# Dequantisation in the first stage alone, and the bf16 parts of the point weights made by GpSimd

## What is computed

```
x = x + xattn0(layernorm(x), ctx, ctx, Wq, bq, Wk, bk, Wv, bv, Wo, bo)
x = x + ffn0(layernorm(x), w_freq_real, w_freq_imag, bias)
x = x + xattn1(layernorm(x), ctx, ctx, w_value, b_value, w_off, b_off, w_attw, b_attw, w_out, b_out)
x = x + ffn1(layernorm(x), w_gate, w_up, w_down)
```

```
s = max(max|w| over the block / 7, 1e-12)
wq = clip(round(w / s), -8, 7) * s
```

## Time and profile before

| what | value |
|---|---|
| median of three runs | 871.84 us (866.13, 871.84, 871.96) |
| the profiled execution | 868.69 us |
| its span | 866.2 us |
| its mean granted TensorE clock | 0.941 |
| busy: TensorE, VectorE, ScalarE, GpSimd | 727.4, 639.0, 465.5, 249.8 us |

### The profile page before, as it was taken

How to read it: one execution, slowest core, us unless ns; L and a number is a source line. 1 busy time by engine, 2 the same in 40 slices (tenths; PEclk the granted TensorE clock), 3 DMA queues, 4 the chain that set the end, 5 groups by cost and what they waited for, 6 DMA issues and landing times.

```text
span 866.2 us, 10711 instructions
## 1 busy us (share of the span) xinstructions
PE 727.4 (84%) x3599; PEld 485.6 (56%) x3599; DVE 639.0 (74%) x1184; ACT 465.5 (54%) x818; POOL 249.8 (29%) x198
## 2 busy tenths in 40 slices
PE   4999998799977788767999987999979990039998
PEld 4878886578766567523455553444434440018887
DVE  3577799966798579955999975877569997993333
ACT  2444455455334668855655512344379959934441
POOL 3000000576784112365676720000023320000000
PEclk9999999799999999889999997999999995559999
DMA  8900000050143300000000000000014339501111
GB/s 279 349 12 1 1 1 0 1 135 1 30 139 85 35 1 1 2 1 1 2 2 1 1 2 0 1 0 1 0 73 163 158 147 403 219 0 37 49 52 58
DMA packets 32122, 52.87 MB, mean 61 GB/s; under 512 B 3523, under 2 KB 27331, under 8 KB 30918
## 3 DMA queue, kind: packets, MB, share of 16 engines
q1 hardware_dynamic: 30256, 50.62, 17.7%
q10 hardware_dynamic: 1814, 1.59, 0.6%
HBM read 35.34 MB, written 16.84 MB: 60 GB/s over the span
## 4 chain that ended last, share of the span: by engine, by line
PE 41%; ACT 11%; DVE 8%; issue 4%; DMA 1%; POOL 0%; SPq 0%; DVEq 0%; ACTq 0%; POOLq 0%
PE pair L1544 10%; PE pair L1591 10%; PE pair L1472 4%; PE pair L1440 4%; PE pair L1455 3%; DVE wide L2085 3%; PE pair L1483 2%; ACT upq L1081 2%; ACT g2q L1087 2%; PE pair L1332 2%; PE pair L1335 2%; ACT wide L1050 1%; DVE peak L1997 1%; PE pair L1569 1%; DMA ups<-up_far 1%
## 5 line engine op out<-in xcount | busy, mean ns | idle before, releaser
L1932 DVE SCALAR_TENSOR_TENSOR hat<-pair,hat 128x1024 f32<-128x1024 f32 x64 | 78.0, 1218 | 29.5 <-ACT hat L970 18.2
L970 ACT ACTIVATE hat<-pair 128x1024 f32<-128x1024 f32 x64 | 65.5, 1024 | 60.9 <-PE pair L1440 60.9
L1569 PE MATMUL pair<-xqs,wuT 128*128 128x512 f32 x192 | 84.6, 601 | 4.7 <-ACT up_stage L1037 4.7
L1544 PE MATMUL pair<-xqs,wgT 128*128 128x512 f32 x192 | 85.4, 603 | 0.0
L1591 PE MATMUL pair<-wdT,hid 128*128 128x256 f32 x384 | 83.1, 379 | 0.4 <-DVE hid L2133 0.4
L723 POOL TENSOR_TENSOR hat<-hat 128x1024 f32<-128x1024 f32 x30 | 70.7, 2357 | 41.3 <-DVE hat L1932 41.3
L1591 PEld LDWEIGHTS pair<-wdT,hid 128*128 128x128 f32 x384 | 72.9, 190 | 11.1 <-DVE hid L2133 1.2
L1569 PEld LDWEIGHTS pair<-xqs,wuT 128*128 128x128 f32 x192 | 36.8, 194 | 51.3 <-issue 51.1
L1152 PE MATMUL pair<-wT,ft_sb 128*128 128x256 f32 x256 | 63.8, 392 | 0.0
L623 POOL TENSOR_TENSOR rstd<-lnt,half 128x8 f32<-128x8 f32 (+2 forms) x15 | 26.4, 1760 | 129.5 <-DVE lnt L1635 129.5
L1102 ACT ACTIVATE hid<-wide,unit 128x768 f32<-128x768 f32 x32 | 32.5, 1026 | 57.2 <-DVE hid L2133 43.7
(11 more groups left out here) (243 smaller groups left out, 1711.8 us busy)
## 6 DMA issues: line engine op xcount, KB each, us to landing
up_far<-up_stage SPq DMA_DIRECT2D x24, 512.0 KB, 2.6
ups<-up_far SPq DMA_DIRECT2D x8, 1536.0 KB, 6.9
x_sb<-in_x_dram SPq DMA_DIRECT2D x8, 512.0 KB, 7.4
c_sb<-in_ctx_dram SPq DMA_DIRECT2D x8, 512.0 KB, 8.7
ctx<-in_ctx_dram SPq DMA_DIRECT2D x32, 128.0 KB
out_dram<-x_sb SPq DMA_DIRECT2D x16, 256.0 KB, 2.1
ctx<-in_ctx_dram SPq DMA_DIRECT2D x16, 126.0 KB
four<-in_c_four_dram SPq DMA_DIRECT2D x1, 1280.0 KB, 6.6
```

Of the source, the lines that this page charges most:

```text
L970: nc.scalar.activation(ramp(n), sides_of(n)[:].rearrange("p i t -> p (i t)"), ACT.Relu).then_inc(relu_done, 1)
L1544: last = mm(bank[2 + oc][:], wgT[:, c, oc * 128:(oc + 1) * 128], xqs[:, s, c, :], start=(c == 0), stop=(c == DC - 1))
L1569: last = mm(bank[2 + oc], wuT[:, c, oc * 128:(oc + 1) * 128], xqs[:, t % 2, c, :], start=(c == 0), stop=(c == DC - 1))
L1932: V.scalar_tensor_tensor(ramp(n), sides_of(n)[:].rearrange("p i t -> p (i t)"), 0.0, ramp(n), ALU.max, ALU.add).then_inc(hat_done, 1)
```

## The change

First, the list of ticks of the 32 dequantisation halves. Before it runs from tick 8 to 38 with seven halves in ticks 32 to 38; after from 5 to 31. Ticks 16 to 19 have two halves each instead of one; 5, 6, 7, 12, 15 and 20 gain one; 22 loses its one, 29 and 30 lose one each.

Second, ScalarE's `first_part` and `second_part` are gone with their eight calls each. GpSimd makes both roundings with a copy, ahead of its own subtraction, and takes over the waits. The calls of `first_residual` and `second_residual` keep their places.

```diff
-DEQ_TICKS = [t for t in range(8, 60) for _ in range(1 if t % 8 in (4, 6, 7) or t < 22 or t >= S3 else 2)
-             if not (t < 22 and t % 8 in (4, 6, 7))][:B]
+DEQ_TICKS = [t for t in range(5, B) for _ in range(2 if t % 8 < 4 and t >= 16 else 1) if t not in (14, 22, 30)][:B]
...
             def first_residual(g):
 
+                pool.wait_ge(ccx_ready, g + 1)
+                if g == NG - 1:
+                    pool.wait_ge(tail_turned, turned_by(g - 2))
+                elif g >= 2:
+                    pool.wait_ge(parts_turned, g - 1)
+                nc.gpsimd.tensor_copy(part_rows(g, 0), ccx_rows(g)).then_inc(hi_done, 1)
                 pool.wait_ge(hi_done, g + 1)
                 pool.wait_ge(w63_ready, g + 1)
                 nc.gpsimd.tensor_tensor(ccx_rows(g), ccx_rows(g), part_rows(g, 0), ALU.subtract).then_inc(res_done, 1)
 
             def second_residual(g):
 
+                pool.wait_ge(res_done, g + 1)
+                nc.gpsimd.tensor_copy(part_rows(g, 1), ccx_rows(g)).then_inc(mid_done, 1)
                 pool.wait_ge(mid_done, g + 1)
                 nc.gpsimd.tensor_tensor(part_rows(g, 2), ccx_rows(g), part_rows(g, 1), ALU.subtract).then_inc(lo_done, 1)
...
-                for tick, step in ((2, exponent), (12, keep_rows), (8, second_part), (6, first_part)):
+                for tick, step in ((2, exponent), (12, keep_rows)):
...
-            first_part(NG - 2)
             for k in range(PAIRS // 2):
                 relu(k)
...
-                if k == 2:
-                    second_part(NG - 2)
-                if k == 5:
-                    first_part(NG - 1)
-                if k == 7:
-                    second_part(NG - 1)
```

More of the change, by code:

```diff
@@ L906, in exponent @@
                 nc.scalar.activation(te[:], te[:], ACT.Exp).then_inc(exp_done, 1)
-            def first_part(g):
-                act.wait_ge(ccx_ready, g + 1)
-                if g == NG - 1:
-                    act.wait_ge(tail_turned, turned_by(g - 2))
-                elif g >= 2:
-                    act.wait_ge(parts_turned, g - 1)
-                nc.scalar.activation(part_rows(g, 0), ccx_rows(g), ACT.Copy).then_inc(hi_done, 1)
-            def second_part(g):
-                act.wait_ge(res_done, g + 1)
-                nc.scalar.activation(part_rows(g, 1), ccx_rows(g), ACT.Copy).then_inc(mid_done, 1)
             def keep_rows(g):
```

## The result

The changed kernel takes 861.38 us (median of 4 runs, 859.39 to 862.86), the kernel before 870.46 us (4 runs, 866.13 to 871.96). The ratio is 0.990, with a 95% interval from 0.987 to 0.993: faster by 1.0%, at the edge of what a measurement of this kernel tells from no change. The profiled execution of the changed kernel took 862.86 us with a span of 860.1, against 868.69 and 866.2: 5.8 us less in all, 6.1 in the span. In the rows after, the lines of the TensorE and VectorE code are 13 lower than before (L1120 is the old L1133, L1772 the old L1785).

The account below looks back on a forecast made before the run. TensorE was taken to bound the first stage, VectorE the second until 169 us, TensorE the fourth with VectorE as full. Terms -6.5 + 0.4 = -6.1 gave 862.6 profiled, 865.7 from the median; forecast 864.0, between them, range 856 to 872.

Parts of the forecast that it names:

- rival A: Fourth stage: VectorE not held as forecast, no lag, sampling starts 2.4 us earlier, 861 us; chance 20%.
- Part 1, the gain of 7.8: Second stage, blocks 3 to 8: without dequantisation the five ticks go at TensorE's pace, 9.15 instead of 16.95 us.
- I charged 0.3: Second stage: VectorE's own peaks in ticks 38 and 39 exceed the lead of its four buffers by about 0.3 us.
- Part 1, the price of 1.0: First stage: double halves in ticks 16 to 19 make VectorE late at tick 21; TensorE waits once, 1.0 us more.
- Rivals B and C: Former (15%): GpSimd, ScalarE or a clock fall limits the second stage, 866; latter (10%): first stage pays 3 us, 866.
- Part 2, the cast at 0.55: Fourth stage: one f32 to bf16 cast of 512 elements on GpSimd was taken to last 0.55 us.
- Part 2, the holds of 2.5 a group: Fourth stage: GpSimd's casts and subtractions hold VectorE 2.5 us a group, 0.9 above its slack of 1.6.
- Part 2, +0.4 at the start of the sampling: TensorE's 2.42 us wait goes, but VectorE's late first hat takes its place: +0.1 to +0.4 us.
- I had VectorE 2.3 us late: End of fourth stage: groups 2 to 4 put VectorE 2.6 us behind, less 0.3, so 2.3 at 353 us.
- I had counted 0.3 there: Fourth stage: VectorE was taken to be 0.3 us ahead after group 1, deducted from its later lag.
- For ScalarE nothing is won: Fourth stage's steady loop: removing the casts gains ScalarE nothing, since they stood behind its copies, off the loop.
- Rival D: Fourth stage: GpSimd casts cost 1.16 us, holds exceed VectorE's slack by 2.5 a group, 872.8 us; chance 10%.

Follow-up runs that it names:

- part 1 alone: The kernel before with only the new dequantisation ticks, casts still on ScalarE: 864.42 us (8 runs), again 864.26 us (10 runs).
- part 2 alone: The changed kernel with the old dequantisation ticks, so only the casts moved to GpSimd: 867.65 us (12 runs), ratio 0.9979.
- four late halves: The changed kernel with single halves in ticks 16 to 19, the last four halves in second-stage ticks 46, 50, 54 and 58: 860.49 us, ratio 0.9881.

## Why the prediction was right

I predicted 864.0 (856 to 872) and 862.6 for the profiled execution; 861.38 and 862.86 were measured. The direction, the range and the main term hold, and one small term had the wrong sign. That the profiled execution came out 0.3 from its number is luck: it lost 1.8 us by its second fall of the clock. And the median lies at rival A's 861, nearer than at my 864.0, so the time alone would have spoken for A; what speaks against it is below.

**Part 1, the gain of 7.8.** Right. From block 3's inverse product to block 8's it is 9.97 us now (159.94 to 169.91), 16.95 before: 6.98 less, where the prediction had 7.8. The group's two products took their 0.45, but 0.55 of VectorE waits was left (0.35 and 0.20; I charged 0.3), and one short transpose more. The blocks before block 3 differ from execution to execution: from block 0's inverse product to block 3's it takes 6.91 and 6.29 us with the old ticks, 5.20 to 7.86 with the new, so nothing there can be put down to the change. Over all profiles block 8's inverse product comes 165.5 us after the first transform with the old ticks (166.21 and 164.85) and 158.9 with the new (158.42 to 159.58 in nine profiles). That is 6.6 less with the price at tick 22 paid, where the prediction had 6.5, and about 7.5 without it, my 7.8 - 0.3. That seven halves moved elsewhere in the same stage give the same gain shows that the place was the cost.

**Part 1, the price of 1.0.** Right, in place and size: one wait of 0.92 at the tick that was named, and with single halves in ticks 16 to 19 it is gone.

**Rivals B and C.** Both fall. In the second stage TensorE waited for no GpSimd result, with GpSimd 7.2 and 8.1 us of 10 busy, and the clock was 1.00 from 160 to 180 us. No later tick of the first stage waited.

**Part 2, the cast at 0.55.** Low by 0.15: 0.69 and 0.73 in the stage. VectorE did not pay for it by its duration: 0.24 for an added cast.

**Part 2, the holds of 2.5 a group.** Too large. The places were right (L1827, L1637, L1831). Their sizes by the rows are 0.80 (1.22 against 0.42), 0.29 to 0.39 (0.69 against 0.40 or 0.30), and 0.85 (1.14 against 0.29 for the same line at 359.07, free), so 2.0 instead of 2.5. VectorE's clean work of 6.9 to 7.0 and these make 8.9 to 9.0, and the group came out at 8.87: 0.29 over TensorE's 8.58, and not 0.9. Two holds were taken too large by the same step, the whole duration of the GpSimd operation as its price: the second cast's (0.55, measured 0.3 to 0.4) and the second subtraction's (1.1, measured 0.85).

**Part 2, +0.4 at the start of the sampling.** Wrong in sign, by two steps. The first is VectorE's lag. I had VectorE 2.3 us late there, and it was not late at all. Counted back from TensorE's first product of the sampling, the last group of weights that VectorE begins in the fourth stage starts (te) 5.42 us before it, 5.29 in the kernel before. VectorE lost 0.29 in each of the three groups of 8.87, but the group ahead of them took 8.70 us, where the kernel before needs 9.68 with its own holds and a wait of 0.83 for TensorE; I had counted 0.3 there.

The second step is what the start of the sampling waits for. GpSimd's first sum waits for VectorE's second hat in every profile; in both of the timelines below it starts within 0.1 us of that hat's end. First the kernel before, then the changed one:

```profile
360.09 0.39 PE L1440 MATMUL pair<-rows,sel 64*128 64x512 bf16 x2
...
363.07 1.17 DVE L1840 TENSOR_TENSOR te<-off,ts 128x256 f32<-128x256 f32 x1
...
365.90 1.09 POOL L717 TENSOR_TENSOR w63m<-w63T,mask 128x512 f32<-128x512 f32 x1
366.13 1.01 DVE L1844 TENSOR_SCALAR tx<-tx 128x256 f32<-128x256 f32 x1
...
367.32 1.21 DVE L1932 SCALAR_TENSOR_TENSOR hat<-pair,hat 128x1024 f32<-128x1024 f32 x1
...
368.62 2.36 POOL L723 TENSOR_TENSOR hat<-hat 128x1024 f32<-128x1024 f32 x1 [1.62 <-DVE hat L1932]
```

```profile
353.32 0.39 PE L1427 MATMUL pair<-rows,sel 64*128 64x512 bf16 x2
...
357.86 1.03 POOL L724 TENSOR_TENSOR w63m<-w63T,mask 128x512 f32<-128x512 f32 x1
...
359.07 0.29 DVE L1831 TENSOR_SCALAR tx<-tx 128x256 f32<-128x256 f32 x1
...
359.54 1.22 DVE L1919 SCALAR_TENSOR_TENSOR hat<-pair,hat 128x1024 f32<-128x1024 f32 x1
```

VectorE's first hat comes 3.91 us after TensorE's first product, where it came 4.17 after: 0.26. Between its two hats VectorE needs 2.31 us instead of 3.06: 0.75. Nearly all of that is one operation. Before, GpSimd's product for the edges (L717) was under way when VectorE came to L1844, which took 1.01; now GpSimd, which has no longer to wait for ScalarE's cast ahead of its subtractions, is done with that product (at 358.89) before VectorE comes to L1831, and it takes 0.29. Together that is D's 1.0. TensorE's wait of 2.42 was not what the first sum waited for.

Nor was ScalarE. Its first hat does come earlier, 1.99 us after TensorE's first product instead of 3.03, since two casts no longer stand ahead of it, and "For ScalarE nothing is won" did not hold at the loop's end. But with every cast twice it comes as early (1.98) and the sum comes at 8.98, and with the first six groups on ScalarE it comes at 2.52 and the sum at 9.01. In both of them GpSimd's edge product ends 7.4 and 7.6 us after TensorE's first product, 5.6 in the changed kernel, and VectorE's operations between the hats are held.

So part 2 is worth -1.0 at the first sum and -0.4 to -1.0 at the thirteenth, not +0.4. Rival A was right that no lag comes, though for another reason than it gave, since VectorE was held; its 2.4 us did not come, since the wait that goes was not the one that bound.

The Trainium skill (SBUF — State Buffer, Who interferes with whom) has the port pair locked for the length of an instruction, and by it I put the holds. The trace agrees on which operations are held, and that reductions pass: 0.68 for the sum L1853 beside the first cast, as without one. For the size, the measured net 0.24 for an added cast decides. The rows fit an operation being held only for what is left of the cast when it arrives: L1637 came 0.14 after the start of a cast of 0.69 and ended 0.14 after the cast's end. What the added casts met was not followed one by one.

**Rival D.** Excluded by the doubled casts: even four casts a group keep TensorE's fourth stage at 58.02 us.

**The sum.** By the traces -6.6 and -0.4 to -1.0, so -7.0 to -7.6, where the prediction had -6.1: part 1 as forecast, part 2 with the wrong sign. The profile that was shown first gave 6.1; against a single profile of the kernel before its stretch A is 7.3 shorter and its stretch E 1.8 longer, both in part by chance. The medians over all runs say 870.1 (52 runs) for before, 864.4 (18) with part 1 alone, 867.6 (12) with part 2 alone, and 861.4 (16) with both: 8.7 for both, 5.7 for part 1 and 2.5 to 3.0 for part 2.

**What stays open.** The 1.5 to 2.5 us by which part 2's share in the medians is above what its traces show. The mean clock was 0.9436 with both parts and 0.9412 with part 1 alone; by the 0.58 us for 0.001 this makes 1.4 us. Whether part 2 makes the falls of the clock rarer or these 16 and 18 runs were uneven by chance is not settled: a variant that read 864.28 in one timing read 862.16 in the next. The variant with the first six groups on ScalarE, which read 861.80 where its trace has D at 9.01, was timed once and stays unexplained. That four late halves beat the changed kernel is shown for stretch A and the wait at tick 22 alone (212.11 against 212.83 to 213.70), not in the whole time.

## What to carry to other kernels

Deferrable work of an engine goes where another engine sets the pace; what it costs is read from the stretch in which it stands, and a few tens of microseconds later the same instructions, even at twice their duration, can be free (four halves here; seven cost 0.87). A wait that a change removes is worth only what the next in line leaves of it: TensorE's 2.42 us went, but the first sum waited for VectorE, and what it gained came from one hold that no longer fell between two hats. Where executions of one kernel differ by more than the effect sought, cut the traces at fixed marks, compare the pieces, take more than one profile of either side, and look whether a gain at one mark is still there at a later one; the medians of two kernels here contradicted their traces, and one of the two fell by 2 us when it was timed again.

## What the runs showed of the hardware

The granted clock (1.00 is the level of 2.4 GHz, 0.50 that of 1.2, values between them are stretches with both) falls at places that differ from one execution to the next of the same kernel on the same work: it was 0.77 between 380 and 390 us in one profile of the changed kernel, 1.00 in the next, and 0.57 between 370 and 380 in the third. Timed runs of the kernel before spread over 10 us (864.83 to 874.75) with clocks from 0.933 to 0.945.

A cast from f32 to bf16 of 128 x 512 on GpSimd took 0.60 to 0.81 us, against 0.63 to 0.68 for the same on ScalarE, and 1.15 to 1.35 for a two-input subtraction of that size. An added cast cost VectorE's queue 0.24 net. Dequantisation operations of VectorE went from 0.31, 0.31 and 0.46 us, with GpSimd idle, to 0.83, 0.61 and 0.91 with GpSimd's products running (four halves late, 182.25 us).
